# Expert weights of a graph and mixture layer: up matrices in two transfers of six and five tiles, one down block asked for earlier

## The reference

```
xn = layernorm(x)
q, k, v = xn @ wq.T + bq, xn @ wk.T + bk, xn @ wv.T + bv
q2, k2, v2 = q @ wiq.T + biq, k @ wik.T + bik, v @ wiv.T + biv      # 16 heads of 64
gnn = softmax(q2 k2 / 8 + mask(edges)) v2 @ wo.T + bo
mix = layernorm(xn + linear_attention(xn @ mq, xn @ mk, xn @ mv) @ mo) * gamma + beta
x1  = x + gnn + mix
xf  = layernorm(x1)
scores = sigmoid(xf @ gate.T);  sel = top2(scores + bias)            # 8 experts
routed = sum over selected e of  square(relu((xf * score) @ up[e].T)) @ down[e].T   # 1408 hidden, bf16
out = x1 + routed + square(relu(xf @ shared_up.T)) @ shared_down.T
```

## Time and profile before

| | us |
|---|---|
| median of 3 runs (lowest, highest) | 357.88 (357.31, 358.4) |
| the profiled execution, its own time | 357.72 |
| span of the profiled execution | 356.3 |
| PE busy | 319.4 |
| DVE busy | 111.4 |
| ACT busy | 58.9 |
| POOL busy | 34.7 |

### The profile page before, as it was taken

The page is one execution under the profiler, slowest core; times in us unless marked ns, Lnnn a source line. Parts: engine busy times, 40 slices in busy tenths (PEclk is TensorE's granted clock), DMA queues, the critical chain, the costliest instruction groups (busy, mean ns, idle before and its releaser), DMA issues.

```text
span 356.3 us, 3258 instructions
## 1 busy us (share of the span) xinstructions
PE 319.4 (90%) x1312; PEld 161.4 (45%) x1312; DVE 111.4 (31%) x246; ACT 58.9 (17%) x113; POOL 34.7 (10%) x63
## 2 busy tenths in 40 slices
PE   4999998999999999999989999899898995473985
PEld 4344334334443343433354565533455673241564
DVE  6608535501143439200632313200322221101111
ACT  1410000001003010200020042300322322111131
POOL 0510110111110110211110010000001030000000
PEclk9999999999999999999999999999999998867899
DMA  7999999999999999999999999999999999999997
GB/s 301 383 358 311 391 335 315 355 348 317 422 318 376 394 278 424 267 420 326 313 360 311 216 422 339 220 217 217 220 212 219 217 217 217 212 220 208 211 212 155
DMA packets 9112, 104.90 MB, mean 294 GB/s; under 512 B 1136, under 2 KB 1608, under 8 KB 2828
## 3 DMA queue, kind: packets, MB, share of 16 engines
q0 software_dynamic: 7920, 97.52, 95.0%
q1 hardware_dynamic: 880, 7.05, 4.9%
q10 hardware_dynamic: 300, 0.16, 0.2%
HBM read 150.48 MB, written 0.39 MB: 423 GB/s over the span
## 4 chain that ended last, share of the span: by engine, by line
PE 68%; DMA 25%; DVE 3%; ACT 2%; issue 1%; another core or an unknown queue 0%
PE bank L852 32%; DMA stage<-in_expert_up 13%; PE bank L1039 9%; PE bank L1014 8%; PE bank L989 5%; PE bank L1084 5%; DMA ring<-in_mat_mv 4%; DMA ring<-in_mat_wik 4%; DMA ring<-in_mat_wo 4%; PE bank L995 3%; PE bank L979 1%; PE bank L823 1%; ACT xn L453 1%; PE bank L860 1%; DVE xn L785 1%
## 5 line engine op out<-in xcount | busy, mean ns | idle before, releaser
L852 PE MATMUL bank<-ring,xnt 128*96 128x512 f32 x224 | 100.1, 604 | 1.4 <-DMA ring<-in_mat_mv 0.7
L852 PEld LDWEIGHTS bank<-ring,xnt 128*96 128x96 f32 x224 | 36.3, 166 | 60.0 <-issue 59.0
L1039 PE MATMUL bank<-stage,hbuf 128*96 128x512 bf16 (+5 forms) x242 | 44.8, 343 | 12.5 <-DMA stage<-in_expert_down 10.2
L1014 PE MATMUL bank<-stage,hbuf 128*96 128x512 bf16 (+1 forms) x192 | 43.1, 375 | 7.0 <-DMA stage<-in_expert_up 7.0
L852 PE MATMUL bank<-ring,stage 128*96 128x512 f32 x96 | 42.2, 594 | 0.4 <-DMA ring<-in_mat_wik 0.4
L1039 PEld LDWEIGHTS bank<-stage,hbuf 128*96 128x96 bf16 x242 | 26.9, 130 | 29.0 <-issue 16.7
L1014 PEld LDWEIGHTS bank<-stage,hbuf 128*96 128x96 bf16 x192 | 23.5, 128 | 22.3 <-issue 10.6
L798 DVE TENSOR_TENSOR acc<-acc_t,acc 96x512 f32<-96x512 bf16 (+5 forms) x22 | 11.9, 543 | 57.9 <-ACT acc_t L478 57.6
L852 PEld LDWEIGHTS bank<-ring,stage 128*96 128x96 f32 x96 | 15.3, 163 | 23.6 <-issue 23.5
L453 ACT ACTIVATE xn<-bank 96x512 bf16<-96x512 f32 (+2 forms) x26 | 14.5, 559 | 63.1 <-PE bank L1014 56.8
L785 DVE TENSOR_TENSOR xn<-xn 96x512 bf16<-96x512 bf16 (+1 forms) x24 | 9.6, 399 | 44.3 <-ACT xn L453 44.3
(11 more groups left out here) (165 smaller groups left out, 215.3 us busy)
## 6 DMA issues: line engine op xcount, KB each, us to landing
stage<-in_expert_up POOLq DMA_DIRECT2D x4, 2816.0 KB, 33.3
stage<-in_expert_down POOLq DMA_DIRECT2D x4, 2816.0 KB, 39.8
stage<-in_expert_down POOLq DMA_DIRECT2D x6, 1408.0 KB, 16.5
stage<-in_expert_up POOLq DMA_DIRECT2D x6, 1024.0 KB, 13.9
ring<-in_mat_wq SPq DMA_DIRECT2D x2, 2048.0 KB, 11.1
ring<-in_mat_wv POOLq DMA_DIRECT2D x2, 2048.0 KB, 11.2
ring<-in_mat_wiq POOLq DMA_DIRECT2D x2, 2048.0 KB, 13.0
ring<-in_mat_wik POOLq DMA_DIRECT2D x2, 2048.0 KB, 13.6
```

Source lines behind the costliest of these rows:

```text
L852: ins = mm(bank[BANKS[m] + h][0:N, :], tiles(src)[:, k, :], w[:, k, :], start=(k == 0), stop=(k == KT - 1))
L1014: ins = mm(bank[4 + j][0:N, 0:c1 - c0], tiles(xe)[:, k, :], w[:, k, :], start=(k == 0), stop=(k == KT - 1))
L1039: ins = mm(bank[j % 4][0:N, 0:c1 - c0], tiles(e_h)[:, t, :], w[:, t, :], start=(t == 0), stop=(t == TT - 1))
```

## The change

The up matrices of experts 0 to 2 were three transfers of four, four and three tiles; now they are two, of six and five. The table has twelve entries in place of fifteen, with new counts. In the order of issue, expert 0's two down blocks are asked for at 6 and 12 instead of 9 and 13, expert 1's at 25 and 30 instead of 29 and 32, expert 2's up at 37 and 38 instead of 37, 39 and 42. The waits on the up semaphores count one transfer less.

```
 FIRST_LOADS = [(e, m, x0, x1) for e in range(3) for m, x0, x1 in
-               [(0, 0, 4), (0, 4, 8), (0, 8, 11), (1, 0, HALF * TT), (1, HALF * TT, D * TT)]]
-FIRST_AT = [0, 3, 6, 9, 13, 16, 21, 24, 29, 32, 37, 39, 42, 44, 44]
+               [(0, 0, 6), (0, 6, 11), (1, 0, HALF * TT), (1, HALF * TT, D * TT)]]
+FIRST_AT = [0, 4, 6, 12, 16, 21, 25, 30, 37, 38, 44, 44]
...
-                        if n == 10:
+                        if n == 8:
                             pool.wait_ge(pv_psum, 2)
                             pool.wait_ge(mvec_t_psum, 2)
...
-            expert(0, 0, HALVES, 32, None, None, None, None)
+            expert(0, 0, HALVES, 16, None, None, None, None)
...
-            expert(1, 1, HALVES, 32, 16, None, (out_taken, 1, 2), None)
+            expert(1, 1, HALVES, 16, 16, None, (out_taken, 1, 2), None)
...
-                expert(i * 3 + 2, 2, HALVES, turn + 48, turn + 32, None, (added, at + 6, at + 6), None)
-                expert(i * 3 + 3, 0, HALVES, turn + 48, turn + 16, None,
+                expert(i * 3 + 2, 2, HALVES, turn + 32, turn + 32, None, (added, at + 6, at + 6), None)
+                expert(i * 3 + 3, 0, HALVES, turn + 32, turn + 16, None,
```

More of the change, by code:

```diff
@@ L202, in gps_layer @@
         part_landed = [sem(f"part_landed{j}") for j in range(len(FINE))]
-        FIRST_LANDED = [up_landed[0], up_landed[0], part_landed[4], part_landed[2], part_landed[3],
-                        up_landed[1], up_landed[1], part_landed[0], down_landed[1], part_landed[1],
-                        up_landed[2], up_landed[2], up_landed[2], down_landed[2], down_landed[2]]
+        FIRST_LANDED = [up_landed[0], part_landed[4], part_landed[2], part_landed[3],
+                        up_landed[1], part_landed[0], down_landed[1], part_landed[1],
+                        up_landed[2], up_landed[2], down_landed[2], down_landed[2]]
         out_landed = sem("out_landed")
@@ L1089, in _ @@
                 at, turn = i * ROUND, i * 16
-                expert(i * 3 + 2, 2, HALVES, turn + 48, turn + 32, None, (added, at + 6, at + 6), None)
-                expert(i * 3 + 3, 0, HALVES, turn + 48, turn + 16, None,
+                expert(i * 3 + 2, 2, HALVES, turn + 32, turn + 32, None, (added, at + 6, at + 6), None)
+                expert(i * 3 + 3, 0, HALVES, turn + 32, turn + 16, None,
                        (out_taken, at + 5, at + 6), None)
-                expert(i * 3 + 4, 1, FINE, turn + 48, turn + 32, turn + 16,
+                expert(i * 3 + 4, 1, FINE, turn + 32, turn + 32, turn + 16,
                        (out_taken, at + 7, at + 8), at + 8)
```

## The result

The changed kernel took 361.29 us in the median of 4 runs (360.56 to 362.72), the kernel before 357.62 in 4 runs beside it. The ratio is 1.010, with a 95% interval of 1.007 to 1.014: slower by 3.7 us, where no change was forecast. The profiled execution took 361.00, its span is 359.7.

A forecast was written before the change was run, and what follows sets the result against it. The prediction took one queue of loads on POOL, never dry, to bound the kernel. The profiled 357.72 us plus 0.3, for expert 3's up and all later loads starting later, gave 358.0, no change; range 357.1 to 359.2.

The forecast's parts named there:

- What bounds the kernel: POOL's queue of loads never runs dry, and its end sets the end of the kernel.
- Merging the transfers: Up loads before 213 us: three transfers fewer in a full queue gain 0 to 0.3 us, 0.1 taken.
- The rival of a fixed cost in a full queue: Each transfer costs 1.5 us even in a full queue; three fewer give 353.2 us; chance 0.02.
- Moving loads, and a PE that is 4.15 us late: Halves land later behind loads put ahead; PE is 6.0 us late at mk's second half, 4.15 at shared up.
- The head start: Time from issue to landing on POOL's queue with nothing ahead, beyond the load's own duration: 3.3 us taken.
- So expert 3's up, and every load behind it, starts at 217.45 + 3.3 = 220.75 instead of 220.47: 0.3 us later: Expert 3's up, issued at 217.45, starts 3.3 us after issue, and all later loads move by 0.3 us.
- the two places don't add up: Of two late issues on POOL's queue, time lost at the first gives the second a fuller queue.
- the first place: Expert 2's first piece, issued at 159.2 instead of 154.04, with 2.8 us of queue left instead of 8.0.
- the sum: Whole kernel: 357.72 us of the profiled execution plus 0.3 gives 358.0, no change.
- the second place: Expert 3's up matrix, issued at 217.45 instead of 213.30, with 2.9 us of queue left instead of 7.2.
- the sum's own case: Expert 3's up issued at 217.45 with 2.9 us of queue left, starting 0.3 us later.
- The slower rival, "the queue runs dry before expert 3's up": At expert 3's up, 4.3 to 4.5 us from issue to start gives 359.0 to 359.2 us; chance 0.21.

The follow-up runs named there:

- the first trace: The profiled execution of the changed kernel as first measured, nothing further altered: 361.00 us.
- the run with the other table: Changed kernel, ups still in two pieces, with table counts that keep every half within PE's slack: 357.93 us, ratio 1.001 to the kernel before.
- the spare matmuls: Changed kernel with eight spare 128 x 128 matmuls on PE before wiv's and before mk's second half: 359.52 us, ratio 1.006 to the kernel before.
- the second trace: The changed kernel, unchanged, profiled again: 362.35 us in one run.
- expert 3's up held to 217.32: Kernel before, with POOL held at expert 3's up until PE finished expert 0's first down block: 358.81 us, ratio 1.003.
- the run with the block at 26: Changed kernel with expert 1's first down block asked for at 26 instead of 25, behind mk's second half: 358.49 us, ratio 1.002 to the kernel before.
- the run with three pieces: Changed kernel with expert 2's up again in three pieces, at 37, 39 and 42: 361.92 us, ratio 1.013 to the kernel before.

## Why the prediction was wrong

**What bounds the kernel: right.** One queue of loads sets the end; the 3.3 us by which expert 3's up lands late in the first trace are carried to the end unchanged.

**Merging the transfers, 0 to 0.3 us gained, 0.1 taken: not contradicted**, by the run with the other table (0.1% slower, with 0 in its interval); a gain so small can't be told from none. The rival of a fixed cost in a full queue, which would have gained 4.5 us, is out.

**Moving loads, and a PE that is 4.15 us late: right** in the first trace (4.31 at expert 3's up) and with the spare matmuls (4.31). But it was only the least lateness. The step took every half for 6.9 us, whatever PE had done before it. After a wait of 2.4 us the half took 8.8, and where no later wait swallowed this, PE was 7.5 us late. This counts for the second trace; in the first PE was as late as forecast, and the loss came all the same.

**The head start, 3.3 taken: nearly right**, 2.9 to 3.2 measured where the queue had run empty or nearly so.

**"So expert 3's up, and every load behind it, starts at 217.45 + 3.3 = 220.75 instead of 220.47: 0.3 us later": this step failed.** Expert 3's up landed 3.3 us later in the first trace and 3.5 in the second. The step reckoned with one loss, the head start less the depth by the last landing, and at one place, since "the two places don't add up". At the first place, expert 2's first piece, this gives 0.5 us (a head start of 3.3 less the 2.8 left); the first trace lost 2.3 there with 2.9 left, and 1.5 more at shared up's second part, which the sum had at nothing. That alone made the load ahead of expert 3's up 3.3 us late, so that the second place was not shallow at all (6.1 us left) and the 217.45 + 3.3 of the step never came into play. In the second trace something was lost at both places.

What the step lacks, as far as it is known: it took the queue for one server that is late only by its last landing. It is 16, and in the kernel before six of them finished expert 3's up 1.9 us or more ahead of its landing. By an estimate from this one transfer, a queue with 2.8 us left by the last landing has only about 1 us left on the engines ahead, less than the head start. With expert 3's up held to 217.32, the sum's own case, the landing was on time to 0.3 us, as computed, all 16 finished within 1 us, and the time still rose by 1.15 us. That the engines ahead lose their lead, and that a stall of one engine then moves a later landing, is the reading that fits these rows and those of the run with the block at 26; it is not proved.

**The slower rival, "the queue runs dry before expert 3's up",** came nearest, with a chance of 0.21. It had the right mechanism, a queue that runs short at a late issue, but named one place only, at which the first trace lost nothing. It was priced at 1.3 to 1.5 us on a longer head start, and at 2.5 with a PE one microsecond later. The head start was not longer; PE was later in the second trace; and the loss of the lead had no price at all.

**What stays open.** In the first trace expert 2's first piece lost 2.3 us with 2.9 left, in the run with three pieces 1.9 with 3.0 left, in the run with spare matmuls, issued 0.1 later, some 0.7. No run says why. Shared up's second part then landed 1.5 us late, more than the one instruction packet of 0.9 us in that stretch. And the clock's share of the 3.7 us is open.

## What to carry to other kernels

In a kernel whose end is set by one full queue of loads, the order of that queue is free only within the slack of whoever issues the next loads: find the landings for which a busy engine has no slack (here wiv's, mq's and mk's second halves), and let nothing be put in front of them. Count the depth of the queue at each issue by the engine that is furthest ahead, not by the last landing: here 4.3 us by the last landing cost nothing where only that issue was late, 2.8 us cost about one. And a short wait of PE can be dearer than its length, since the clock may fall in it: here 1.7 us on top of a wait of 2.4.

## What the runs showed that I had not expected

- The 16 DMA engines finished one transfer of 2816 KB spread over about 2 us, and an instruction packet behind it moved no landing. After the queue had been shallow once, all 16 finished within 1 us, and with the same packet the landing behind moved by 0.9 us.
- After a wait of 2.4 us in PE's stretch of fp32 matmuls the granted clock read 0.66 over 4 us, and 16 matmuls took 8.8 us instead of 7.1. This did not come every time: after a wait of 1.26 us in the same run, and after one of 2.38 us in the second trace of the changed kernel, the half took 7.08.
- Time from issue to landing on a GpSimd queue that was empty or had 0.5 us left was 2.9 to 3.2 us above the load's own duration, and a load of 2816 KB with only 2.8 us left ahead of it landed without delay.
